# Graph attention over 8192 nodes: keys loaded in 4 KB runs, their row halves turned by DMA, three masks of the first tile on POOL, and another split of the last tile

## What is computed

```python
def _L0_gnn_ref(qs, ks, adj):              # qs: 8192x128, ks: 8192x128, adj: 8192x8192 of 0 and 1
    scores = jnp.einsum('nd,md->nm', qs, ks)
    scores = jax.nn.leaky_relu(scores, negative_slope=0.2)
    scores = jnp.where(adj > 0, scores, -9e15)
    attn = jax.nn.softmax(scores, axis=1)
    return jnp.einsum('nm,md->nd', attn, ks)

h = jnp.maximum(_layernorm(x, axis=-1), 0.0)
return x + _L0_gnn_ref(h, L0_gnn_ks, adj)  # x: 8192x128 f32, adj: int32
```

## Time and profile before

| what | us |
|---|---|
| median of three runs | 1605.21 |
| lowest, highest | 1602.86, 1609.5 |
| the profiled execution's own time | 1603.36 |
| its span | 1601.6 |
| TensorE matmuls busy | 1561.6 (98%) |
| VectorE busy | 1423.2 (89%) |
| ScalarE busy | 1350.2 (84%) |
| POOL busy | 1332.6 (83%) |

### The profile page before, as it was taken

The page is one execution under the profiler, slowest core; times in us unless marked ns, Lnnn a source line. Parts: engine busy times, 40 slices in busy tenths (PEclk is TensorE's granted clock), DMA queues, the critical chain, the costliest instruction groups (busy, mean ns, idle before and its releaser), DMA issues.

```text
span 1601.6 us, 37520 instructions
## 1 busy us (share of the span) xinstructions
PE 1561.6 (98%) x13186; PEld 1155.7 (72%) x13186; DVE 1423.2 (89%) x2528; ACT 1350.2 (84%) x2017; POOL 1332.6 (83%) x1352
## 2 busy tenths in 40 slices
PE   5699999999999999999999999999999999999998
PEld 3377777777777777777777777777777777777776
DVE  6998998998998998998898998899899899898895
ACT  6688888888888888888888888888888888888886
POOL 1588888888888888888888888888888888888887
PEclk9999999999999999999999999999999999999999
DMA  8699999999999999999999999999999999999996
GB/s 275 176 251 273 275 280 283 283 286 271 285 272 276 270 281 286 278 269 276 287 279 294 271 286 275 282 266 281 272 276 284 278 287 281 287 283 283 270 267 119
DMA packets 695098, 434.52 MB, mean 271 GB/s; under 512 B 617088, under 2 KB 625280, under 8 KB 694912
## 3 DMA queue, kind: packets, MB, share of 16 engines
q1 hardware_dynamic: 694912, 432.12, 111.2%
HBM read 276.82 MB, written 4.19 MB: 175 GB/s over the span
## 4 chain that ended last, share of the span: by engine, by line
PE 93%; DMA 1%; DVE 1%; POOL 1%; ACT 0%; issue 0%; POOLq 0%; DVEq 0%; ACTq 0%
PE ps_out L391 27%; PE ps_out L392 14%; PE ps_scores L365 13%; PE ps_scores L367 13%; PE ps_scores L366 13%; PE ps_T L376 12%; DMA keys_in<-keys_in 1%; PE ps_out L343 0%; PE ps_out L390 0%; POOL keys_in L319 0%; ACT scores L467 0%; DVE mask L578 0%; PE ps_out L389 0%; POOL keys_in L317 0%; DVE keys L567 0%
## 5 line engine op out<-in xcount | busy, mean ns | idle before, releaser
L319 POOL TENSOR_TENSOR keys_in<-scores,keys_in 128x512 f16<-128x512 f32 x576 | 728.8, 1265 | 46.5
L596 DVE CUSTOM_DVE_ANT_0 scores<-ps_scores,mask,minus_scale 128x1024 f32<-128x1024 f32 x512 | 653.8, 1277 | 17.0 <-PE ps_scores L367 2.1
L458 ACT ACTIVATE scores<-scores 128x1024 f32<-128x1024 f32 x512 | 537.6, 1050 | 79.5 <-DVE pair_min L596 79.5
L317 POOL CAST keys_in<-scores 128x512 f16<-128x512 f32 x576 | 463.7, 805 | 164.4 <-ACT scores L467 160.0
L467 ACT ACTIVATE scores<-scores,neg_max 128x1024 f32<-128x1024 f32 x512 | 583.1, 1139 | 0.0
L391 PE MATMUL ps_out<-keys,keys_in 128*128 128x256 f16 x2240 | 431.4, 273 | 1.1 <-DMA keys_in<-keys_in 1.1
L605 DVE TENSOR_TENSOR probsT_lo<-ps_T,probsT_hi 128x512 f16<-128x512 f32 x448 | 308.3, 688 | 126.9 <-ACT probsT_hi L475 118.1
L365 PE MATMUL ps_scores<-keysT_hi,hT_hi 128*128 128x512 f16 x1024 | 389.6, 381 | 17.2 <-DVE keysT_lo L560 10.6
L392 PE MATMUL ps_out<-keys,keys_in 128*128 128x128 f16 x2240 | 400.8, 219 | 0.0
L475 ACT ACTIVATE probsT_hi<-ps_T 128x512 f16<-128x512 f32 x448 | 264.7, 591 | 151.2 <-PE ps_T L376 146.8
L366 PE MATMUL ps_scores<-keysT_lo,hT_hi 128*128 128x512 f16 x1024 | 389.6, 380 | 0.0
(11 more groups left out here) (52 smaller groups left out, 829.5 us busy)
## 6 DMA issues: line engine op xcount, KB each, us to landing
adj_in<-in_adj_dram SPq DMA_DIRECT2D x512, 512.0 KB, 5.3
keys_in<-keys_in SPq DMA_TRANSPOSE x576, 5.5
x_in<-in_x_dram SPq DMA_DIRECT2D x16, 256.0 KB, 4.3
keys_in<-in_L_gnn_ks_dram SPq DMA_DIRECT2D x8, 512.0 KB, 7.4
out_dram<-out_tile SPq DMA_DIRECT2D x16, 256.0 KB, 3.8
```

Of the source, the lines that this page charges most:

```text
L317: nc.gpsimd.tensor_copy(half[:, 0:BLOCK], probs(t, b)).then_inc(half_hi_ready, 1)
L319: nc.gpsimd.tensor_tensor(half[:, BLOCK:2 * BLOCK], probs(t, b), half[:, 0:BLOCK], ALU.subtract) \
L458: nc.scalar.activation(s, s, ACT.Prelu, alpha=1.0 / SLOPE).then_inc(leaky_ready, 1)
L596: nc.vector.tensor_tensor_reduce(out=score_pair(q, p), in0=ps_scores[:, slots, :].rearrange("p s k -> p (s k)"), in1=mask[:, (p // 2) % 2, ...
```

## The change

1. The keys are loaded so that partition q gets eight rows in a row (q * 8 to q * 8 + 7 of a pair), a run of 4 KB. ScalarE's copy into keysT writes its columns with a stride of eight elements, so that keysT has the keys in their order.
2. The keys by rows (keys, now [P, 2, CHUNKS, D]: all low halves, then all high ones) are no longer made by ScalarE and VectorE: SP issues sixteen transposing DMAs of keysT_hi and keysT_lo, one per pair and half. The 128x256 matmul reads its moving operand in two runs.
3. Masks 1, 2 and 3 of tile 0 are made by POOL in two operations each.
4. In the last tile five blocks (1, 3, 5, 7, 9) are turned by DMA and eleven by TensorE, and VectorE makes their high halves in ScalarE's place.

```diff
+    LAST_BY_DMA = (1, 3, 5, 7, 9)
...
-        keys = sbuf("keys", [P, CHUNKS, 2 * D], fp16)
+        keys = sbuf("keys", [P, 2, CHUNKS, D], fp16)
...
+        def by_dma(t):
+            return LAST_BY_DMA if t == TILES - 1 else BY_DMA
+
+        def by_pe(t):
+            return tuple(b for b in range(BLOCKS) if b not in by_dma(t))
...
-            return t * len(BY_PE) + sum(c < b for c in BY_PE)
+            return sum(len(by_pe(s)) for s in range(t)) + sum(c < b for c in by_pe(t))
...
-            key_chunks = ks.rearrange("(c p) d -> p c d", p=P)
+            key_pairs = ks.rearrange("(b q c) d -> b q c d", q=P, c=PER_PAIR)
...
-                    sp.wait_ge(keys_lo_ready, keys_under(R_SLOTS + n))
+                    sp.wait_ge(keysT_done, BLOCKS)
+                    sp.wait_ge(scale_steps, PAIRS)
                 sp.dma_start(turned[:, n % D_SLOTS, :, :], halves[:, n % R_SLOTS, :], transpose=True) \
                     .then_inc(turned_in[n % D_SLOTS], 16)
+
+            def turn_keys(p, part):
+                source, ready = (keysT_hi, keysT_hi_ready) if part == HI else (keysT_lo, keysT_lo_ready)
+                sp.wait_ge(ready, p + 1)
+                sp.dma_start(keys[:, part, p * PER_PAIR:(p + 1) * PER_PAIR, :], source[:, pair_cols(p)],
+                             transpose=True).then_inc(keys_turned[p], 16)
 
             load_x(0)
             for p in range(PAIRS):
                 c = slice(p * PER_PAIR, (p + 1) * PER_PAIR)
-                sp.dma_start(keys_in[:, c, :], key_chunks[:, c, :]).then_inc(keys_loaded[p], 16)
+                sp.dma_start(keys_in[:, c, :], key_pairs[p]).then_inc(keys_loaded[p], 16)
...
+                        if i == -1:
+                            turn_keys(j // 2, HI)
+                            if j // 2 < 4:
+                                turn_keys(j // 2, LO)
+                        if i == 0 and j // 2 < 4:
+                            turn_keys(4 + j // 2, LO)
...
+            def make_first_mask(k):
+
+                pool.wait_ge(adj_loaded[2 * k], 16)
+                pool.wait_ge(adj_loaded[2 * k + 1], 16)
+                pool.wait_ge(mask_ready, k)
+                if k >= 2:
+                    pool.wait_ge(masked_ready, 2 * k - 2)
+                m = mask[:, k % 2, :]
+                nc.gpsimd.tensor_scalar(m, adj_in[:, k, :], 1.0, 0.0, ALU.min, ALU.max).then_inc(clamped, 1)
+                pool.wait_ge(clamped, k)
+                nc.gpsimd.tensor_scalar(m, m, -MASKED, MASKED, ALU.mult, ALU.add).then_inc(mask_ready, 1)
+
             normalise(0)
+            make_first_mask(1)
+            make_first_mask(2)
...
+                    if j == 7 and i == -1:
+                        make_first_mask(3)
...
-                    pe.wait_ge(keys_lo_ready, b // 2 + 1)
+                    pe.wait_ge(keys_turned[b // 2], 32)
...
+                both = o[:, 0:2 * D].rearrange("p (s d) -> p s d", s=2)
...
-                nc.tensor.matmul(o[:, 0:2 * D], hi_part, keys[:, c, :], start=(b == FIRST and k == 0), stop=False)
-                return nc.tensor.matmul(o[:, D:2 * D], lo_part, keys[:, c, D:2 * D], start=False, stop=False)
+                    nc.tensor.matmul(o[:, D:2 * D], lo_part, keys[:, HI, c, :], start=False, stop=False)
+                    return nc.tensor.matmul(both, hi_part, keys[:, :, c, :], start=False, stop=True)
+                nc.tensor.matmul(both, hi_part, keys[:, :, c, :], start=(b == FIRST and k == 0), stop=False)
+                return nc.tensor.matmul(o[:, D:2 * D], lo_part, keys[:, HI, c, :], start=False, stop=False)
...
-                nc.scalar.activation(keysT[:, cols(b)], ps_T[:, b % 2, :], ACT.Copy).then_inc(keysT_copied, 1)
+                dst = keysT[:, pair_cols(b // 2)].rearrange("d (q c) -> d c q", c=PER_PAIR)
+                nc.scalar.activation(dst[:, b % 2 * PER_BLOCK:(b % 2 + 1) * PER_BLOCK, :],
+                                     ps_T[:, b % 2, :].rearrange("d (c q) -> d c q", c=PER_BLOCK), ACT.Copy).then_inc(keysT_copied, 1)
 
             def split_keysT_hi(p):
                 act.wait_ge(keysT_copied, 2 * p + 2)
                 nc.scalar.activation(keysT_hi[:, pair_cols(p)], keysT[:, pair_cols(p)], ACT.Copy,
                                      scale=key_scale[:, :]).then_inc(keysT_hi_ready, 1)
-
-            def split_keys_hi(p):
-                c = slice(p * PER_PAIR, (p + 1) * PER_PAIR)
-                nc.scalar.activation(keys[:, c, D:2 * D], keys_in[:, c, :], ACT.Copy, scale=key_scale[:, :]) \
-                    .then_inc(keys_hi_ready, 1)
...
-                    if i == -1 and j % 2 == 1:
-                        split_keys_hi(j // 2)
-                    split = behind(i, j, T_LAG, BY_PE, this, prev)
-                    if split:
+                    split = behind(i, j, T_LAG, by_pe, this, prev)
+                    if split and split[0] < TILES - 1:
                         split_probs_hi(*split)
...
-            def split_keys_lo(p):
-                c = slice(p * PER_PAIR, (p + 1) * PER_PAIR)
-                dve.wait_ge(keys_hi_ready, p + 1)
-                nc.vector.scalar_tensor_tensor(out=keys[:, c, 0:D], in0=keys_in[:, c, :], scalar=key_scale[:, 0:1],
-                                               in1=keys[:, c, D:2 * D], op0=ALU.mult, op1=ALU.subtract) \
-                    .then_inc(keys_lo_ready, 1)
...
+            def split_last_hi(t, b):
+                n = nth_pe(t, b)
+                dve.wait_ge(T_done, n + 1)
+                dve.wait_ge(out_done, n - T_SLOTS + 1)
+                nc.vector.tensor_copy(probsT_hi[:, n % T_SLOTS, :], ps_T[:, n % 2, :]).then_inc(T_hi_ready, 1)
...
-                    if i == 0 and j % 2 == 0:
-                        split_keys_lo(p)
-                    split = behind(i, j, T_LAG, BY_PE, this, prev)
-                    if more and j in (4, 8, 12):
+                    split = behind(i, j, T_LAG, by_pe, this, prev)
+                    if more and i >= 0 and j in (4, 8, 12):
...
+                    if split and split[0] == TILES - 1:
+                        split_last_hi(*split)
```

More of the change, by code:

```diff
@@ L129, in gat_kernel @@
         keysT_lo_ready = sem("keysT_lo_ready")
-        keys_hi_ready = sem("keys_hi_ready")
-        keys_lo_ready = sem("keys_lo_ready")
+        keys_turned = [sem(f"keys_turned{p}") for p in range(PAIRS)]
+        clamped = sem("clamped")
         bn_done = sem("bn_done")
@@ L185, in nth_pe @@
         def nth_pe(t, b):
-            return t * len(BY_PE) + sum(c < b for c in BY_PE)
+            return sum(len(by_pe(s)) for s in range(t)) + sum(c < b for c in by_pe(t))
         def nth_dma(t, b):
-            return t * len(BY_DMA) + sum(c < b for c in BY_DMA)
+            return sum(len(by_dma(s)) for s in range(t)) + sum(c < b for c in by_dma(t))
         def score_pair(t, p):
@@ L203, in gat_kernel @@
             .rearrange("p (s k c) -> p s k c", s=D_SLOTS, k=2 * PER_BLOCK)
[L205 to L206 removed]
+        LO, HI = 0, 1
         block = ctx.enter_context(nc.Block())
@@ L224, in behind @@
             t, b = (i, j - lag) if j >= lag else (i - 1, j - lag + BLOCKS)
-            return (t, b) if b in kind and (this if t == i else prev) else None
+            return (t, b) if (this if t == i else prev) and b in kind(t) else None
         @block.sync
         def _(sp):
-            key_chunks = ks.rearrange("(c p) d -> p c d", p=P)
+            key_pairs = ks.rearrange("(b q c) d -> b q c d", q=P, c=PER_PAIR)
             def load_x(g):
@@ L270, in step @@
                             load_adj(q, p)
+                        if i == -1:
[4 more added lines that the diff above has]
+                            turn_keys(4 + j // 2, LO)
                     for b in (0, 1):
-                        turning = behind(i, j, TURN_LAG - b, BY_DMA, this, prev) if j % 2 == 1 else None
+                        turning = behind(i, j, TURN_LAG - b, by_dma, this, prev) if j % 2 == 1 else None
                         if turning:
@@ L314, in split_half @@
                 else:
-                    pool.wait_ge(keys_lo_ready, keys_under(n))
+                    pool.wait_ge(keysT_done, BLOCKS)
+                    pool.wait_ge(scale_steps, PAIRS)
                 half = halves[:, n % R_SLOTS, :]
@@ L326, in step @@
                     for b in (0, 1):
-                        split = behind(i, j, LO_LAG - b, BY_DMA, this, prev) if j % 2 == 1 else None
+                        split = behind(i, j, LO_LAG - b, by_dma, this, prev) if j % 2 == 1 else None
                         if split:
@@ L386, in accumulate @@
                 o = ps_out[:, t % 2, :]
+                both = o[:, 0:2 * D].rearrange("p (s d) -> p s d", s=2)
                 c = b * PER_BLOCK + k
                 if b == LAST and k == PER_BLOCK - 1:
-                    nc.tensor.matmul(o[:, D:2 * D], lo_part, keys[:, c, D:2 * D], start=False, stop=False)
-                    return nc.tensor.matmul(o[:, 0:2 * D], hi_part, keys[:, c, :], start=False, stop=True)
```

(14 more changed lines are left out.)

2 lines of the change are left out of this document (removed).

## The result

| | before | after |
|---|---|---|
| median, lowest, highest of 20 runs each (us) | 1603.82, 1602.45, 1609.5 | 1600.34, 1595.11, 1602.91 |
| ratio, 95% interval | | 0.9974 [0.9966, 0.9981] |
| profiled execution, its span | 1603.36, 1601.6 | 1600.33, 1598.5 |

About 3.5 us were gained (0.26%), within the 0.5% that I had called "the same"; 10.8 were forecast. The time lies inside the range of 1588 to 1605.

What follows compares the result with a forecast made beforehand. TensorE was taken to bound the middle and nearly all of the last tile, VectorE step 0. Terms 1.2 - 0.8 + 10.0 + 0.4 = 10.8 us off 1603.36 or 1605.21 gave 1592.6 or 1594.4; forecast 1594, range 1588 to 1605.

Steps and rivals of the forecast that it cites:

- leaves the steady step alone: Middle tiles: the change touches only start, step 0 and end; steady steps stay 24.1 us, apart from one operand's form.
- part 3: Step 0: row halves of keys by transposing DMA remove eight VectorE operations; 32.83 to 22.8 us, 10.0 gained.
- Behind it step 1 is TensorE's as before: Step after the shortened step 0: TensorE still bounds it, at 23.5 us.
- part 1: Start: keys in 4 KB runs, copy taken as 0.60 us; key_scale at 20.8 instead of 22.02, 1.2 us gained.
- part 2: Between key_scale and tile 0's neg_max: three masks on POOL, 1.9 us per operation, mutual exclusion with VectorE; 0.8 us lost.
- rival (a): Key loading: strided copy is slow, 0.42 us more per pair, transposes end 3.2 us later; 1597.6 us, chance 0.20.
- my layout: Hand-made schedule from key_scale to tile 0's neg_max: nearly every POOL operation between two lo parts, 29.8 us against 29.0.
- Rival (b): Tile 0's masks: POOL's operations are slow, 4.6 us each gives 1610.6 us, 10 us each gives 1643; chance 0.13.
- Rival (d): Step 0 takes 27 us, not 22.8, as ScalarE's chain or exclusion replaces the eight operations; 1598.6 us, chance 0.07.
- Part 4: Last tile: five blocks turned by DMA, four more on TensorE, high halves on VectorE; 0.4 us gained.
- Rival (c): Matmuls on keys: moving operand in two runs costs extra, at 3 ns each 1606 us; chance 0.05.
- Rival (e): More gained than reckoned: TensorE's clock stays up in step 0 and masks fit better; 1589 us, chance 0.05.

Runs made afterwards that it cites:

- e14: The changed kernel with every second adjacency load of tiles 1 to 63 cut to its first half: 1592.31 us, ratio 0.9922.
- e16: Changed kernel with 512-byte key runs, plain copy, keys' low parts turned earlier, six turned blocks in tile 0, a quarter of adjacency not loaded: 1592.04 us.
- e15: The kernel before with the same quarter of the adjacency not loaded as in e14: 1603.54 us, ratio 0.9990.
- e3: The changed kernel with the keys loaded in 512-byte runs and copied into keysT without a stride: 1599.39 us, ratio 0.9970.
- e8: The changed kernel with the keys in 2 KB runs and ScalarE's copy at a stride of four elements (16 bytes): 1603.21 us, one run.
- e2: The changed kernel with the three masks of tile 0 back on VectorE: 1599.79 us, ratio 0.9972.
- e1: The changed kernel with its last tile as before (nine blocks turned by DMA, high halves on ScalarE): 1598.23 us, ratio 0.9962.

## Why the prediction was wrong

**The step that failed** is the opening's "leaves the steady step alone", and in part 3 "Behind it step 1 is TensorE's as before": the sum passes what is won ahead of tile 2 on to the end whole, so it puts the cost in the steady tiles at nothing. They took back 3.75 us.

I read TensorE's 23.50 of 23.50 us as a bound with room beside it and never asked how much room the transfers had. The same rows gave DMA 1.09 against 0.70 in step 0: the DMA engines had a third less to do per us in step 0 than later, and this pause filled the store of turned blocks. In tiles 0 and 1 before has its turned blocks 3.4 to 7.5 us early; after, with a step 0 that is 8 us shorter, 0 to 3.4; e14, from tile 2 on, never less than 2.2 (all worked out from each block's landing and the first matmul on it). The steady tiles don't build such a reserve up: in before it shrinks to 1.7 to 3.6 us in tile 24.

Where it is gone, an irregular moment becomes a wait of TensorE, and that is how after's lead fell from 6.36 us at tile 5 to 2.15 at tile 22 (at tile 30 before loses 0.4 itself). Each such wait gives the transfers time, and in tile 24 after's blocks are 2.0 to 4.2 us early, so the losses stop. That the load is the cause is shown by e14; this last account of single waits is read from the traces and not tested. How much is lost differs from run to run, and in e14 to e16, with less to load, the runs hardly scatter.

By terms, 7.7 us of the 10.8 are missing in the profiled execution: 3.7 in part 1, 1.9 in part 3, 4.0 in step 1 and the steady tiles; part 2 and the end gave 1.9 more than forecast. In e14 against e15 the kernels differ by 11.2 us, close to the forecast, but in part by luck: from key_scale to the end the terms are -1.8, +1.0, +10.9, 0.0 for the middle and +0.7 for the end, where I had 1.2, -0.8, 10.0, 0 and 0.4. What e14 bears out is that a middle with room costs nothing, and the size of part 3.

**Part 1** failed as rival (a) says: the copy takes 1.10 us (0.60 before), where its upper bound was 1.02. Instead of 1.2 gained, 2.5 were lost. The rate was right (416 GB/s, 414 foretold), and without effect. I took the copy from the row of the same instruction with another output pattern; e3 has 0.60 with the plain copy (its loads differ too, but the copy reads PSUM and not what they write), so the stride is the cause. The Trainium skill (SBUF — State Buffer, Door 1: The DMA port swizzle, the note on cachelines) warns of this stride of 8 fp32, and the trace agrees; but by the note 4 fp32 are free, and e8's stride of 4 cost the same 1.08 to 1.15 us. The sum of the start missed 3.7 us by it. Still, the median would hardly have been better: e3 has the plain copy and 0.9970.

**Part 2** had the mechanism and the price right. POOL's operation called at 42.41 has to let the lo part of 41.85 to 43.12 end, and is done at 44.88, 1.76 us later (forecast 1.9); the next lo part, called at 44.25, takes 1.70 instead of 1.27. But VectorE lost only about 2.8 us by such meetings (4.11 against 2.48 for the first two, then 0.27, 0.43 and 0.43), since add_mask ran beside POOL more often than in my layout: 1.0 gained instead of 0.8 lost, and e2 has the same 0.95. Rival (b) is refuted. By the Trainium skill (GPSIMD Engine Reference, section 3.1, Elementwise) the estimate was 1.95 us; the trace has 1.76, 10% less.

**Part 3's** own size was 10.0; measured 8.1, and 10.9 where the transfers have room (32.83 - 21.96). The missing 2.8 us is the one wait at 70.54, for a turned block and not, as I feared, for the keys. Rival (d) comes near the total (1598.6) for a reason that isn't the one found, which is luck: step 0 was longer than forecast neither by ScalarE's chain nor by exclusion, but by the DMA stream.

**Part 4** came out as reckoned: 0.5 gained (0.4 forecast, and e1 loses 0.5 without it), TensorE 10.96 of 11.00 us, and a high half at the price of a lo part, from VectorE's timeline (answering to the earlier trace rows):

```profile
1578.51 0.69 DVE L631 CAST probsT_hi<-ps_T 128x512 f16<-128x512 f32 x1 [0.78 <-PE ps_T L412]
1579.23 0.69 DVE L636 TENSOR_TENSOR probsT_lo<-ps_T,probsT_hi 128x512 f16<-128x512 f32 x1
```

Rival (c) is refuted: 24.10 us per tile in both kernels where nothing waits, so the moving operand in two runs costs nothing. Rival (e)'s clock was right (1.00 in step 0 instead of 0.90), its total wasn't.

**What I did not have among the rivals** was a second resource close to the bound. The price of the DMA stream could have been bounded from the trace: 4.19 MB of adjacency per tile at 414 GB/s are 10.1 us, and the nine turned blocks share what is left.

## What to carry to other kernels

Ask of a full engine also how much slower the next resource may get: an engine at 100% beside a DMA stream may be two bounds, 1% apart, and the busy share doesn't tell (1.15 with TensorE as the bound, and 1.15 with the transfers as the bound). How early the transfers land before their use does tell. A long early step can be a reserve for the stream behind it; shortening it then pays only up to what the stream has to spare, and the rest comes back as small waits over the next tens of tiles, and as scatter. To find the second bound, take work from the full engine: where the period hardly falls (here 0.2 of 3.5 us), the other one is named by the waits that appear. And before a step of one trace is compared with that of another, compare their granted clocks.

## What the runs showed of the hardware that was not expected

- ScalarE's 128x512 fp32 copy out of PSUM takes 0.60 us with its output in one run, and 1.08 to 1.15 us with a stride of 16 bytes as well as with one of 32.
- A transposing DMA of a block (both halves, 256 KB) is dear: taking one of nine out of each tile shortened the period by 1.2 us, where VectorE stopped it. If the adjacency takes 10.1 of the 23.9 us, the nine have at most 13.8, some 1.5 each (an estimate).
- A quarter less of adjacency brought the median landing of a transposing DMA from 5.5 to 4.5 us, and took the scatter of the changed kernel from 7.8 us (20 runs) to 0.5 (4 runs), and that of the kernel before from 7.1 (20 runs) to 1.1 (10 runs).
- The same step 0 ran at mean granted clocks of 1.00 (after) and 0.93 (e2), with TensorE busy 20.28 and 21.91 us for the same work.
